# Linear-attention kernel: key-value products in two groups, two banks scaled into SBUF

## What is computed

```python
def linear_attention(x, Wq, bq, Wk, bk, Wv, bv, g, bb):
    q = gelu(x @ Wq + bq) + 0.21
    k = gelu(x @ Wk + bk) + 0.21
    v = x @ Wv + bv
    q_r, k_r = rope(q), rope(k)                      # 16 heads of 16 channels
    z = 1.0 / (einsum('bhnd,bhmd->bhnm', q, mean(k)) + 1e-06)
    kv = einsum('bhnd,bhne->bhde', k_r, v) / n
    out = einsum('bhnd,bhde->bhne', q_r, kv) * z
    return layernorm(out + x, g, bb)
```

## Time and profile before

| | us |
|---|---|
| median of 3 runs | 1804.67 |
| the profiled execution's own time | 1804.48 |
| its span, first to last instruction | 1802.5 |
| TensorE busy | 1772.3 (98%) |
| VectorE busy | 1483.2 (82%) |
| GpSimd busy | 997.3 (55%) |
| ScalarE busy | 922.5 (51%) |
| share of the chain that ended last | TensorE 92%, VectorE 3%, DMA 2% |

### The profile page before, as it was taken

One profiled execution on the slowest core, in us unless ns is written; L12 is line 12 of the kernel. 1 busy time (PEld: TensorE's weight loads), 2 busy tenths in 40 slices (PEclk: granted clock), 3 DMA queues, 4 the chain that ended last, 5 costly groups with the idle time before them and its releaser, 6 DMA issues.

```text
span 1802.5 us, 42043 instructions
## 1 busy us (share of the span) xinstructions
PE 1772.3 (98%) x17084; PEld 1440.9 (80%) x17084; DVE 1483.2 (82%) x3486; ACT 922.5 (51%) x1741; POOL 997.3 (55%) x775
## 2 busy tenths in 40 slices
PE   9999999999999999999998999999999999999998
PEld 3336788888888888888886988888888888888887
DVE  3667799999999999999997749696979788888887
ACT  4555666777766777766776723332333333332231
POOL 1556999999999999999991022121313121212221
PEclk9999999999999999999999999999999999999999
DMA  7363442122325422323238711010101010101000
GB/s 285 148 255 146 135 113 48 39 70 48 84 49 153 137 65 49 83 49 76 70 92 274 241 62 48 24 47 24 47 24 47 24 48 24 36 35 36 30 7 24
DMA packets 30193, 148.59 MB, mean 82 GB/s; under 512 B 5488, under 2 KB 6320, under 8 KB 20784
## 3 DMA queue, kind: packets, MB, share of 16 engines
q1 hardware_dynamic: 20960, 89.62, 14.1%
q0 software_dynamic: 6272, 46.14, 11.5%
q10 hardware_dynamic: 2768, 10.15, 1.5%
HBM read 80.89 MB, written 31.46 MB: 62 GB/s over the span
## 4 chain that ended last, share of the span: by engine, by line
PE 92%; DVE 3%; DMA 2%; POOL 1%; issue 1%; ACT 1%; ACTq 0%; SPq 0%; DVEq 0%; POOLq 0%
PE bankC L1433 13%; PE bankC L33 7%; PE bankC L32 7%; PE bankC L34 7%; PE ring L32 6%; PE ring L34 6%; PE ring L33 6%; PE bankC L1432 6%; PE big L32 3%; PE big L853 3%; PE big L33 3%; PE big L34 3%; PE ring L873 3%; PE hid_ps L245 3%; PE conv_ps L256 3%; PE big L928 2%
## 5 line engine op out<-in xcount | busy, mean ns | idle before, releaser
L1433 PE MATMUL bankC<-down,act_hi 128*128 128x512 f32 x992 | 353.1, 397 | 0.0
L1432 PE MATMUL bankC<-down,act_lo 128*128 128x256 f32 x868 | 246.2, 284 | 0.0
L1433 PEld LDWEIGHTS bankC<-down,act_hi 128*128 128x128 f32 x992 | 186.3, 188 | 41.9
L1558 DVE TENSOR_TENSOR act_lo<-gel,act_hi 128x512 fp32r<-128x512 f32 x256 | 210.6, 823 | 8.7
L33 PE MATMUL bankC<-aT_lo,up_hi 128*128 128x512 f32 x512 | 199.6, 390 | 0.0
L32 PE MATMUL bankC<-aT_hi,up_hi 128*128 128x512 f32 x512 | 199.5, 390 | 0.0
L34 PE MATMUL bankC<-aT_hi,up_lo 128*128 128x512 f32 x512 | 199.4, 389 | 0.0
L1512 POOL TENSOR_TENSOR hC<-hC,vecC 128x1024 f32<-128x1024 f32 x16 | 38.7, 2416 | 283.9 <-PE turn L1407 283.9
L1518 POOL TENSOR_TENSOR rstdC<-var_epsC,minus_halfC 128x4 f32<-128x4 f32 x47 | 56.1, 1194 | 249.2 <-DVE var_epsC L1586 249.2
L1432 PEld LDWEIGHTS bankC<-down,act_lo 128*128 128x128 f32 x868 | 164.1, 189 | 1.4
L773 POOL TENSOR_TENSOR kr<-kr,kc 128x512 f32<-128x512 f32 x128 | 161.8, 1296 | 0.2 <-DVE kr L1077 0.2
(11 more groups left out here) (211 smaller groups left out, 5224.0 us busy)
## 6 DMA issues: line engine op xcount, KB each, us to landing
qc<-qs POOLq DMA_DIRECT2D x64, 512.0 KB, 6.5
raw_late<-in_AB SPq DMA_DIRECT2D x30, 320.0 KB, 3.8
u<-hA SPq DMA_DIRECT2D x8, 1024.0 KB, 4.8
u_next<-u SPq DMA_DIRECT2D x8, 1024.0 KB, 5.7
hC<-u SPq DMA_DIRECT2D x16, 512.0 KB, 4.2
xC<-in_x SPq DMA_DIRECT2D x16, 512.0 KB, 5.1
out<-w_flat SPq DMA_DIRECT2D x15, 512.0 KB, 2.6
w_flat<-in_AB SPq DMA_DIRECT2D x22, 320.0 KB, 4.2
```

The costliest lines, as they stand in the source:

```text
L1432: e.matmul(bank[:, 0:H], a_lo[:, fb, tok], both[k][:, fb, 0, :], start=False, stop=False)
L1433: m = e.matmul(bank[:, :], a_hi[:, fb, tok], both[k][:, fb, :, :].rearrange("p a h -> p (a h)"), start=fb == 0, stop=fb == FB - 1)
L1558: e.tensor_tensor(a_lo[:, fb, :], g, a_hi[:, fb, :].bitcast(F32), ALU.subtract).then_inc(s_act_lo, 1)
```

## The change

Five edits in `attention_phase`:

1. Banks 2 and 3 are scaled into SBUF: `scale(n, 2)` and `scale(n, 3)` still read PSUM but write to the second half of `qs` (free then), and `add_h` of these two reads that and `yB`. `values(n, 2)` and `values(n, 3)` wait for `scale` and no longer for `add_h`. `rotate_q`, which writes the same part of `qs`, waits for `add_h`.
2. Of `finish`, steps 1 to 6 all come behind `rotate_k` 3; before, step 1 lay ahead of it.
3. In `FINISH`, `turn 2` goes ahead of `add_h 0`, and `scale 3` ahead of `add_h 2`.
4. `key_value(n-1)` and `turn_u(n, 1)` are issued as: block 0 of the products, four transposes, block 1 of the products, four transposes.
5. `outputs(31)` is issued behind the first group of composition products, as their `last`.

```diff
+        HELD = 2
+        apart = lambda i: qs[:, i - HELD, half(1)]
...
-            def turn_u(n, x):
+            def turn_u(n, x, blocks=range(CB)):
...
-                for cb in range(CB):
+                for cb in blocks:
...
             def values(n, u):
-                w.wait_ge(s_y, 4 * (n - 1) + u + 1)
+                if u < HELD:
+                    w.wait_ge(s_y, 4 * (n - 1) + u + 1)
+                else:
+                    w.wait_ge(s_scaled, 4 * (n - 1) + u + 1)
...
-            def key_value(n):
+            def key_value(n, blocks=range(CB)):
...
-                for db in range(CB):
+                for db in blocks:
...
-                m.then_inc(s_kv, 1)
+                if CB - 1 in blocks:
+                    m.then_inc(s_kv, 1)
...
-                    key_value(n - 1)
-                    turn_u(n, 1)
+                    for b in range(CB):
+                        key_value(n - 1, [b])
+                        turn_u(n, 1, [b])
...
             key_value(UNITS - 1)
-            outputs(UNITS - 1)
-            then(e, lambda: None)
+            then(e, lambda: outputs(UNITS - 1))
...
                 w.wait_ge(s_out, n)
+                w.wait_ge(s_y, 4 * (n - 1) + HELD + db + 1)
...
             def scale(n, i):
+                to = out if i < HELD else apart(i).rearrange("p (a n d) -> p a n d", a=TILES, d=HD)
...
-                e.tensor_tensor(out, out, zb, ALU.mult).then_inc(s_scaled, 1)
+                e.tensor_tensor(to, out, zb, ALU.mult).then_inc(s_scaled, 1)
...
             def add_h(n, i):
+                sums = big[i][:, :] if i < HELD else apart(i)
...
-                e.tensor_tensor(heads, big[i][:, :].rearrange("p (a m) -> p a m", a=TILES), heads, ALU.add).then_inc(s_y, 1)
+                e.tensor_tensor(heads, sums.rearrange("p (a m) -> p a m", a=TILES), heads, ALU.add).then_inc(s_y, 1)
...
-            FINISH = [[(turn, 0)], [(turn, 1), (scale, 0)], [(add_h, 0), (turn, 2)], [(scale, 1), (add_h, 1)],
-                      [(turn, 3), (scale, 2)], [(add_h, 2), (scale, 3)], [(add_h, 3)]]
+            FINISH = [[(turn, 0)], [(turn, 1), (scale, 0)], [(turn, 2), (add_h, 0)], [(scale, 1), (add_h, 1)],
+                      [(turn, 3), (scale, 2)], [(scale, 3), (add_h, 2)], [(add_h, 3)]]
...
-                    if n >= 1 and u < 3:
-                        finish(n - 1, u - 1)
+                    if n >= 1 and u == 1:
+                        finish(n - 1, 0)
                 if n >= 1:
-                    for k in range(2, 7):
+                    for k in range(1, 7):
                         finish(n - 1, k)
```

## The result

The changed kernel takes **1851.5 us** (median of 6 runs, 1840.0 to 1859.5) where the kernel before takes 1804.9 (6 runs, 1802.8 to 1808.1): a ratio of 1.025 with a 95% interval of 1.022 to 1.029, so 47 us slower, where 3 us were forecast and the range ended at 1815.5. Its runs are also 20 us apart where those of before are 5 apart. The profiled execution took 1850.0 us, with a span of 1847.6.

What follows compares the result with a forecast made beforehand. TensorE bounds the kernel before at 24.48 us a unit; changed, a VectorE-GpSimd loop gives 24.68. Over 30 units + 6.0, less 3.0 at the end, makes + 3.0 on 1804.48: 1807.5 us, whole range 1798 to 1815.5.

Steps and rivals of the forecast that it cites:

- The one that comes second waits for the other to end: VectorE additions with two SBUF inputs against GpSimd's operations: the later is held until the other ends; VectorE goes on 0.47 behind.
- one unit in nine: Share of units where `add_h` 2 waits one rotation more, 1.26 us; adds 0.14, so 24.68 us per unit.
- the loop: VectorE and GpSimd holding each other at `add_h` 2 and 3: 24.54 us a unit, longer than TensorE's 24.39; chance 0.50.
- Rival 2: `add_h` 2 mostly held through a second rotation: half the units missed, some 24.95 us a unit, 1815.5 us; chance 0.15.
- DMA of weights: In one unit in four it shifts GpSimd by 0.6 us; that unit falls back to TensorE's pace, inside the rounding.
- TensorE waiting for the DMAs of line 807 in most units: Sign of the forecast: the late DMA issue holds TensorE at `outputs`, which waits for the landing 8.4 us behind the issue.
- 1.0 us of room: Slack of the third key projection, which needs the transposed rows after VectorE's work; their shift was priced at nothing.
- Order, and values on scale: TensorE's stalls at the fourth query projection (0.11) and third value product (0.20) go: 24.48 to 24.17 us a unit.
- Two groups: One more change between transposes and 32-column products each way costs TensorE net 0.22 us a unit (0.12 to 0.27).
- The three terms of the transitions: Per unit on TensorE: 0.09 lost into products, 0.12 lost going back, transposes 0.06 slower; 0.27 us in all.
- Last outputs: Behind the attention, composition products fill TensorE's idle time for the DMAs: gain 3.0 us (1.5 to 4.5).
- Rival 1: The held additions fit into VectorE's and GpSimd's slack, TensorE's 24.39 us a unit decides: 1798.7 us, faster; chance 0.20.

Runs made afterwards that it cites:

- e5: Changed kernel with GpSimd's two rotation instructions cut to 64 of 512 columns in every unit but the first, so its result is not computed; 1798.7 us.
- e8: Changed kernel, computing the same, with GpSimd waiting for its own earlier instructions only ahead of each pair of rotations; 1814.0 us.
- e4: Changed kernel without edit 1 (banks 2 and 3 scaled into SBUF); 1820.6 us.
- e1: Kernel before with edit 4 alone (the two groups of products and transposes); 1812.0 us.
- e7: Kernel before with last outputs later, fourth key rotation earlier, finishing steps interleaved, one transpose block ahead of the third value product; no SBUF banks or split; 1790.9 us.
- e2: Kernel before with edit 5 alone (last outputs behind the first group of composition products); 1800.3 us.
- e6: Changed kernel, computing the same, with GpSimd waiting for its own last instruction ahead of each sum of keys and rotation; 1828.4 us.
- e3: Kernel before with edit 1 alone (banks 2 and 3 scaled into SBUF), in the old order of finish; 1866.6 us.
- e9: Changed kernel with its key-value products in one group again; 1846.2 us.

## Why the prediction was wrong, point by point

- **The step that failed** is this one: "The one that comes second waits for the other to end", and from it "where a landing or a bank is that much late, `add_h` 2 waits for one rotation more, 1.26 us. I take one unit in nine". Half of the sentence is right: two SBUF inputs are held by GpSimd, and in half of the units the additions take some 1.55 and 1.78 us and the rotations 1.77 and 1.73. In 13 of those units GpSimd's DMAs are issued 24.61 to 24.68 us apart: that is the loop, forecast as 24.54, with GpSimd's second rotation held 0.47 us and not 0.33. But the addition that misses its turn does not wait for one rotation more; it waits until GpSimd's train has ended, up to four instructions behind the one in which it asked, 3.2 to 6.0 us in all, and this in 15 of 32 units and not in one of nine. The rows it came from the earlier trace rows have single instructions of GpSimd with idle time around them (4.17 us ahead of the one at 1181.93, and 4.55 behind it). They cannot show what happens when the next one is ready, and in the loop GpSimd is busy 23.14 of 24.5 us. Rival 2 had the direction, and half of the units is what came, with the same wrong price: a missed turn at 1.26 us gave it 1815.5.
- **A term put at nothing.** Of the DMA of weights I wrote "that unit falls back to TensorE's pace; this is inside the rounding". Each of these six units was passed over, and its issues lie 27.96 to 28.02 us apart, 3.3 more than the loop.
- The Trainium skill (SBUF — State Buffer, SBUF: two separate sides) says that whichever starts first of a GpSimd instruction and a VectorE instruction with two SBUF inputs gets the shared pair of ports "for the whole instruction; the other fully blocks". The good units agree (1.53 and 1.78 us). The page says nothing on who is next when both are waiting, and here that is where the time went.
- **Where it bites.** I looked for the loop to hold TensorE through the DMAs of line 807. "TensorE waiting for the DMAs of line 807 in most units" did not come: six waits, of 0.4 to 2.5 us. The changed kernel holds TensorE through `split_u` and the third key projection, given 1.0 us of room in the prediction. A delay of up to 5 us on VectorE's side runs through it (30.6 us in 26 waits), and with some of these stalls the clock falls to half. Cutting the long additions alone (e5, e8) took away both.
- **Order, and values on scale:** forecast 0.31 us a unit. Right for the stalls: neither of them is in the changed kernel, and with the held additions gone (e5) the unit is 24.44. What I did not see is that edit 3 without edit 1 makes the stall four times as long (e4).
- **Two groups:** 0.22 was too low, and so was its upper bound of 0.27. e1 has 0.29, and e5 against e7 0.30 (24.44 - 24.14). The three terms of the transitions add up to nearly that (0.27); the 0.05 that the second half was to win back by queued work is not there. With two groups, products and transposes take 2.46 us where they took 2.17 (695.41 - 693.24 in e7). In e5:

```profile
695.53 0.84 PE L917 MATMUL ring<-v,kr 128*32 128x33 f32 x64
696.30 0.66 PE L857 MATMUL big<-identity,yB 128*128 128x128 f32 x4
696.89 0.77 PE L917 MATMUL ring<-v,kr 128*32 128x33 f32 x64
697.58 0.65 PE L857 MATMUL big<-identity,yB 128*128 128x128 f32 x4
697.99 0.47 PE L32 MATMUL ring<-hT_hi,w_second 128*128 128x512 f32 x1
```

  The first half starts 0.77 us ahead of its transposes and the second 0.69, 1.46 together, where the one group of e7 took 1.33 (693.24 to 694.57); the transposes take 0.59 and 0.41, 1.00 where eight in a row took 0.84. The 0.35 us estimated from the drain figure of the Trainium skill (TensorE: Matmul & The Clock Gate, Single matmul latency) is above the 0.29 measured.
- **Last outputs:** forecast -3.0, measured -2.9 in e2's trace. In the changed kernel only -1.2 of it is left (1847.57 - 991.25 against 857.52), since VectorE is late there too: TensorE waits 4.05 us for the first group's operand and then runs it at half clock.
- **Rival 1**, the holds fit into the slack, was priced at 1798.7. e5, where the holds are gone, is at 1798.7; its trace has 3.3 us less in the units ((940.06 - 177.99) / 31 = 24.58) and 2.6 less behind them, where the rival had 2.8 and 3.0. So the price of a kernel without holds stood, though that both come to 1798.7 is luck, and the condition was wrong: with all of GpSimd's work and no long hold (e8) it is 1814.0.

**What stays open.** Why one request is let in and the next, at the same phase, is passed over. Gaps of 0.08 to 0.17 us in GpSimd's train end it (e6, e8); GpSimd's second instruction of a pair, in e8, never passed a waiting addition (11 cases, too few against 6 of 35). Whether the waiting addition asks again only at intervals, or GpSimd has claimed the next turn before its last one ends, no run here tells. Nor was the DMA of weights moved, though the longest holds all stand in its units. The clock's share was not measured by itself either: between 204 and 948 us, in stretches of 24 us, six of the changed kernel's 31 have a mean granted clock under 1.00 (0.93, 0.93, 0.86, 0.97, 0.96, 0.93), which is 0.42 x 24 = 10 us of full clock at most, part of it idle time; the kernel before has none there.

## What to carry to other kernels

A VectorE addition whose two inputs both lay in SBUF was cheap (0.69 us) only where GpSimd had nothing long to do. Where GpSimd works without gaps, count it not as waiting for one instruction but for the whole train, and look for the units in which GpSimd has one thing more to do; keep one of its inputs in PSUM, or leave a gap in GpSimd's queue where the addition comes. And a price read from two single instructions side by side holds for single instructions: before using it, look whether in the new place a third one is waiting. Last, where an engine is late by a tenth of a microsecond, first look for dependent neighbours in its order and for work of the waiting engine that can go ahead; both were free here, and gave 14 us (3 of them at the attention's end) where the banks in SBUF cost 31.

## What the runs showed of the hardware that was not expected

- VectorE's addition with two SBUF inputs was held for 3.2 to 6.0 us in about half of the units: beyond the instruction of GpSimd in which it asked, 2 to 4 more went ahead of it. With gaps of 0.08 or 0.17 us in GpSimd's train (e6, e8) none of 128 took over 1.80 us.
- An instruction of VectorE that reads PSUM and writes SBUF is not held: `scale` into `qs` takes 0.67 us (251.60; 0.665 to 0.684 in all 64), as into PSUM.
- A program with such a race in it scattered by 20 us (1840.0 to 1859.5) and by 19 (e3), though once by 4 only (e9, four runs); the programs without it by 1 to 6 (e1, e2, e4 to e8).
- TensorE's granted clock was 0.50 behind stalls of 2.19 and 2.75 us, and 1.00 behind one of 2.45.
- Splitting one run of 32-column products costs 0.29 us, of which the products themselves take 0.13 and the transposes 0.16 (e5 against e7).
